# Four groups of loads behind the sums trip, and a second operand of 96 rows

## The chip, the cores and the metric

The kernel runs on one core of a Trainium2 chip. The metric is the device time of one execution in microseconds; the time of a kernel is the median of several runs. Beside it there is one profiled execution, from which every row below comes. PE is TensorE, PEld its weight loads, DVE VectorE, ACT ScalarE, POOL GpSimd, SP the engine that issues the DMAs here.

## The reference

Two layers on an image of 48 x 48 = 2304 positions with 256 channels, batch 2. Cut to the two attentions that the change touches:

```python
# layer 0, x normed by groups; 8 heads, hd = 32, values of 64
attn1 = softmax(Q1 @ K1.T * hd ** -0.5)
attn2 = softmax(Q2 @ K2.T * hd ** -0.5)
out = (attn1 - lam * attn2) @ V        # then an RMS norm and a projection
# layer 1, 4 heads of 64
logits = where(causal, q @ k.T * 64 ** -0.5, finfo.min)
attn_out = softmax(logits) @ v
# then a linear recurrence, a gate and an FFN, and a second FFN on the better half of the tokens
```

## The kernel before, in words

The program is a sequence of stages: projection, differential attention (16 pairs of batch and head), a middle stage, causal attention (2 batches of two pairs of heads), recurrence with FFN, the second FFN and the choice of tokens. The change touches the two attentions. Each is written engine by engine, with semaphores between them; the order of the work is that of the program text.

**Differential attention** (`differential_attention`). A head's 2304 queries are cut into NC = 6 chunks of T = 384, the keys into 18 steps of 128. The 96 chunks q run in a hardware loop (`Fori`) of 8 rounds with 12 chunks, two heads, written out in its body; SP's program is written out for all 96. Queries and keys are each split in a high and a low part, and the scores need three products of 32 rows, so qs and ks hold 96 rows of parts and one more row, in which the negative maximum of a query is added (L394 scores, 97 rows; L404 maxima, 96 rows). For a chunk, PE makes 36 score matmuls into three banks (`ring`), ACT takes the exponential (L502) into probs, PE multiplies by the values (L430), POOL and DVE add up the probs (L654, L601). In between PE makes the scores of a chunk ahead once more with the queries on the partitions (`max_pair`, L404), and DVE reduces them to maxima (L582); there are two buffers for these.

The sums of chunk q-1 are inverted during chunk q by a trip of four legs on SP's queue (`invert_sums`): row_sums out to memory (L348), compact in (L350), then DVE's reciprocal (L605), row_factors out (L353), and recip in twice (L357). DVE's `normalise` (L612) then makes normed, which SP stores (L363). In DVE's program L605 stands between reductions of maxima in slot 2 of the chunk.

At q % 6 == 0, ahead of trip and store, SP issues the loads of the next head (`load`): three parts for each of qs and ks and both halves, 12 loads of 288 KB, and the values, one of 576 KB. All count on one semaphore, s_ld, which PE waits for in chunk 4 of the head (slot 4) and DVE in chunk 5 (slot 2).

**Causal attention** (`causal_attention`). A pair of heads z // 6 has six query chunks, chunk c with 3 * (c + 1) steps of 128 keys. The product has two operand pairs: qa and ka with 128 rows, qb and kb with the remaining product of 64 rows; in qb and kb a 65th row, number DH = 64, adds the negative maximum. A score (`score_step`) is L1162 (128 rows) and L1163 (65 rows), on the diagonal also L1165 (mask). A maximum (`max_unit`) is L1179 (128 rows) and L1180 (64 rows: without the row of the maximum), on the diagonal L1182 (mask), reduced by DVE (L1299) from one of three banks. L1191 multiplies probs and values, with two heads in the two halves of 64 columns; L1216 sums up the same way; L1204 (`rows`) turns the maxima, with one column. DVE and ACT write the turned row into row 64 of qb (`place_row`). A planner (`plan`) spreads the 504 maxima units of later chunks over the 252 steps, two to three to a step:

```python
for lap, uz, u in todo[:n]:
    max_unit(b + lap, uz, u)
score_step(b, z, g)
for lap, uz, u in todo[n:n + 1]:
    max_unit(b + lap, uz, u)
if g > 0:
    pv_step(b, z, g - 1)
for lap, uz, u in todo[n + 1:]:
    max_unit(b + lap, uz, u)
```

Ahead of its loop of two rounds (one per batch) PE makes the 24 units of the first two chunks. DVE first sets row 64 of the four kb to one (L1289), then `ones` (L1291) and `ident_bf` (L1293); PE waits for all of these and for its first loads.

Of the kernel before, what the change touches and what calls it, by code (L numbers as in the profile page):

```python
# [6 lines left out]
F32 = mybir.dt.float32  # L7
F32R = mybir.dt.float32r
BF16 = mybir.dt.bfloat16
ALU = mybir.AluOpType  # L10
ACT = mybir.ActivationFunctionType
AX = mybir.AxisListType

P = 128
# [3 lines left out]
N = 48 * 48  # L18
T = 384
NC = N // T  # L20
SUB = T // P
NT = N // P
H0 = 8
HD = 32
VD = 2 * HD
# [213 lines left out]
def differential_attention(nc, qk_hi, qk_lo, v_rows, lambdas, ident, row_sums, row_factors, o_rows):  # L239
# [11 lines left out]
    LOADS = 2 * 2 * PARTS + 1  # L251
    PAIRS = SUB * NC

    SLOTS = 2 * STEPS + 3
# [28 lines left out]
    with ExitStack() as ctx:  # L283
        sb, ps, sem = tools(nc, ctx, "diff")
# [39 lines left out]
        with nc.Block() as block:  # L324
            @block.sync
            def _(sp):
# [7 lines left out]

                def load(n):
                    par, (b, h) = n % 2, divmod(n % HEADS, H0)
                    for j in range(2):
                        for dst, kind, parts in ((qs, 0, (qh, qh, ql)), (ks, 1, (qh, ql, qh))):
                            for r, src in enumerate(parts):
                                sp.dma_start(dst[par][j][r * HD:(r + 1) * HD, :].bitcast(F32),  # L340
                                             src[b * 2 * H0 + kind * H0 + h, j, :, :]).then_inc(s_ld[par], 16)
                    sp.dma_start(vs[par][:, :, 0, :], v_tiles[:, b * NT:(b + 1) * NT, h * VD:(h + 1) * VD]
                                 ).then_inc(s_ld[par], 16)

# [15 lines left out]
                def store(q):  # L360
                    n, c = divmod(q, NC)
                    sp.wait_ge(s_norm, q + 2)
                    sp.dma_start(o_rows[:, n + 1, c * T:(c + 1) * T], normed[:]).then_inc(s_st_o, 16)  # L363
# [4 lines left out]
                for q in range(CHUNKS):  # L368
                    if q % NC == 0:

                        sp.wait_ge(s_pv, q * BATCHES + BATCH)
                        load(q // NC + 1)
                    invert_sums(q - 1)
                    store(q - 1)
                invert_sums(CHUNKS - 1)
# [604 lines left out]
def causal_attention(nc, qk_hi, qk_lo, v_rows, ident, o_t):  # L980
# [4 lines left out]

    HN, DH = 4, C // 4
    PAIRS = HN // 2
    BANKS = 3
# [57 lines left out]
    with ExitStack() as ctx:  # L1046
        sb, ps, sem = tools(nc, ctx, "causal")
        ka = [[sb(f"ka{i}{j}", [P, N], F32R) for j in range(2)] for i in range(2)]
        kb = [[sb(f"kb{i}{j}", [DH + 1, N], F32R) for j in range(2)] for i in range(2)]
        qa = [sb(f"qa{j}", [P, N], F32R) for j in range(2)]  # L1050
        qb = [sb(f"qb{j}", [DH + 1, N], F32R) for j in range(2)]
        vs = [sb(f"vs{i}", [P, NT, 2, DH]) for i in range(2)]
# [26 lines left out]
        with nc.Block() as block:  # L1079
# [64 lines left out]
            def _(pe):  # L1144
# [23 lines left out]
                def max_unit(b, z, u):  # L1168
# [10 lines left out]
                    pe.matmul(to, qa[j][:, queries], ka[par][j][:, keys], start=True, stop=False)  # L1179
                    mm = pe.matmul(to, qb[j][0:DH, queries], kb[par][j][0:DH, keys], start=False, stop=k < c)  # L1180
                    if k == c:
# [64 lines left out]
            def _(act):  # L1246
# [4 lines left out]
                def place_row(b, z):  # L1251

                    c = z % NC
                    act.wait_ge(s_rows, b * SLOTS + z + 2)
                    act.activation(qb[1][DH:DH + 1, c * T:(c + 1) * T], misc[32:33, 0:T], ACT.Copy).then_inc(s_row, 1)

# [26 lines left out]
            def _(dve):  # L1283
# [3 lines left out]
                for par in range(2):  # L1287
                    for j in range(2):
                        ins = dve.memset(kb[par][j][DH:DH + 1, :].bitcast(F32), 1.0)  # L1289
                ins.then_inc(s_ones, 1)  # L1290
# [18 lines left out]
                def place_row(b, z):  # L1309

                    c = z % NC
                    dve.wait_ge(s_rows, b * SLOTS + z + 2)
                    dve.tensor_copy(qb[0][DH:DH + 1, c * T:(c + 1) * T], misc[0:1, 0:T]).then_inc(s_row, 1)

# [898 lines left out]
```

## Time and profile before

| what | us |
|---|---|
| median of 3 runs (6028.88 to 6040.64) | 6037.92 |
| the profiled execution | 6063.87 |
| its span, first to last instruction | 6062.1 |
| PE busy | 5460.9 (90%) |
| DVE, ACT, POOL busy | 3506.3, 2393.7, 3071.3 |
| differential attention, from SP's first load to the last chunk | 229.6 to some 3240 |
| causal attention, PE's first to last matmul | 3634.8 to 4566.7 |

Read the stages apart: the shares of busy time are means over all of them. In a window a row gives busy time of each engine and PEclk, the granted share of TensorE's clock (1.00 is 2.4 GHz, 0.50 is 1.2 GHz). In a timeline the distance between two starts says more of a matmul than its modelled duration, since matmuls overlap.

### The profile page before, as it was taken

The page shows a single profiled execution, that of the slowest core. Times are in us where ns is not written, and L with a number is a line of the kernel's source. Part 1 is how long each engine was busy: PE and PEld are TensorE (multiplying, and loading weights), DVE is VectorE, ACT ScalarE, POOL GpSimd, SP SyncE. Part 2 cuts the span into 40 slices and gives each one's busy share as a digit, 9 for nine tenths or more (in the row PEclk, how much of TensorE's full clock was granted, in tenths as well). Part 3 has the DMA queues.
Part 4 walks back from the last instruction along what each step waited for, and adds up shares of the span by engine and source line. Part 5 has one row for each costly group of instructions (what it writes and reads, how often), then busy time and mean ns, then how long its engine had stood idle before and what let it go on. Part 6 is the DMA issues. An engine that isn't in the chain of part 4 may idle for free. (4 is left out here: it accounts for less than half of the span.)

```text
span 6062.1 us, 84099 instructions
## 1 busy us (share of the span) xinstructions
PE 5460.9 (90%) x23692; PEld 3112.7 (51%) x23692; DVE 3506.3 (58%) x4330; ACT 2393.7 (39%) x5287; POOL 3071.3 (51%) x1607
## 2 busy tenths in 40 slices
PE   8799999999999999999996979999997988897970
PEld 4455555555555555555553434554554555554540
DVE  3477777777777777777774543443443444443228
ACT  3255555555555555555552211322322333332430
POOL 0198888988888988888883102544441000000001
PEclk9799999999999999999997886999998999998995
DMA  6601111101111011111013643112201000000121
GB/s 224 190 16 40 41 42 42 37 19 42 42 42 42 18 39 40 42 41 41 15 41 94 179 147 73 37 37 53 58 16 61 21 21 21 21 10 30 47 92 69
DMA packets 244613, 330.97 MB, mean 55 GB/s; under 512 B 87260, under 2 KB 224754, under 8 KB 234490
## 3 DMA queue, kind: packets, MB, share of 16 engines
q1 hardware_dynamic: 244218, 326.08, 19.4%
q8 instruction: 201, 3.29, 0.2%
q14 instruction: 194, 1.59, 0.1%
HBM read 202.49 MB, written 123.51 MB: 54 GB/s over the span
## 5 line engine op out<-in xcount | busy, mean ns | idle before, releaser
L654 POOL TENSOR_TENSOR diff_run_pool<-diff_run_pool,diff_probs 128x768 f32<-128x768 f32 x1152 | 2235.1, 1940 | 187.8 <-ACT diff_probs L502 100.6
L582 DVE TENSOR_REDUCE diff_maxes<-diff_max 128x1 f32<-128x768 f32 x1752 | 1571.7, 950 | 676.3 <-PE diff_max L404 675.5
L502 ACT ACTIVATE diff_probs<-diff_ring 128x384 f32<-128x384 f32 x3462 | 1398.8, 495 | 956.9 <-PE diff_ring L394 843.0
L430 PE MATMUL diff_out_ps<-diff_probs,diff_vs 128*64 128x384 f32 x6912 | 1272.5, 504 | 0.0
L394 PE MATMUL diff_ring<-diff_qs,diff_ks 97*128 97x384 f32 x3462 | 1076.5, 385 | 19.6 <-issue 10.1
L404 PE MATMUL diff_max<-diff_ks,diff_qs 96*128 96x384 f32 x3504 | 953.9, 354 | 98.8 <-DVE diff_maxes L582 65.0
L394 PEld LDWEIGHTS diff_ring<-diff_qs,diff_ks 97*128 97x128 f32 x3462 | 607.3, 188 | 552.1 <-issue 360.1
L430 PEld LDWEIGHTS diff_out_ps<-diff_probs,diff_vs 128*64 128x64 f32 x6912 | 453.0, 139 | 559.3 <-issue 360.5
L404 PEld LDWEIGHTS diff_max<-diff_ks,diff_qs 96*128 96x128 f32 x3504 | 613.0, 193 | 148.3 <-DVE diff_maxes L582 95.5
L2083 POOL MEMSET pick_before<- 128x128 f32 x1 | 0.2, 204 | 1311.0 <-POOLq L63 1311.0
L1299 DVE TENSOR_REDUCE causal_maxes<-causal_max 128x1 f32<-128x384 f32 x522 | 288.7, 554 | 522.2 <-PE causal_max L1180 316.4
L1377 POOL TENSOR_TENSOR causal_run_sum<-causal_run_sum,causal_probs 128x768 f32<-128x768 f32 x180 | 329.0, 1828 | 275.6 <-ACT causal_probs L1273 275.6
L1273 ACT ACTIVATE causal_probs<-causal_scores 128x384 f32<-128x384 f32 x504 | 228.4, 488 | 588.0 <-PE causal_scores L1163 400.9
L659 POOL TENSOR_TENSOR diff_row_sum<-diff_run_pool,diff_sum_dve 128x768 f32<-128x768 f32 x96 | 176.5, 1839 | 172.9 <-DVE diff_sum_dve L601 164.4
L1179 PE MATMUL causal_max<-causal_ka,causal_qa 128*128 128x384 f32 x522 | 229.2, 439 | 31.9 <-DMA causal_vs<-v_rows 28.1
L1180 PE MATMUL causal_max<-causal_kb,causal_qb 64*128 64x384 f32 x522 | 243.3, 466 | 0.0
L1191 PE MATMUL causal_out_ps<-causal_probs,causal_vs 128*64 128x384 f32 x1008 | 226.9, 531 | 0.0
L1162 PE MATMUL causal_scores<-causal_qa,causal_ka 128*128 128x384 f32 x504 | 217.4, 431 | 0.0
L601 DVE TENSOR_TENSOR diff_run_dve<-diff_probs 128x768 f32<-128x768 f32 x96 | 206.1, 2147 | 0.0
L654 POOL TENSOR_TENSOR diff_run_pool<-diff_probs 128x768 f32<-128x768 f32 x96 | 174.6, 1818 | 53.6 <-ACT diff_probs L502 46.0
L1179 PEld LDWEIGHTS causal_max<-causal_ka,causal_qa 128*128 128x128 f32 x522 | 106.0, 203 | 160.0 <-DVE causal_maxes L1299 105.0
L601 DVE TENSOR_TENSOR diff_run_dve<-diff_run_dve,diff_probs 128x768 f32<-128x768 f32 x96 | 183.0, 1907 | 0.0
(228 smaller groups left out, 5935.9 us busy)
## 6 DMA issues: line engine op xcount, KB each, us to landing
diff_qs<-qk_hi SPq DMA_DIRECT2D x68, 288.0 KB, 7.7
diff_ks<-qk_hi SPq DMA_DIRECT2D x68, 288.0 KB, 10.1
diff_recip<-row_factors SPq DMA_DIRECT2D x194, 96.0 KB, 2.7
o_rows<-diff_normed SPq DMA_DIRECT2D x97, 192.0 KB, 1.8
qk_hi<-proj_hi SPq DMA_DIRECT2D x12, 1536.0 KB, 5.8
qk_lo<-proj_lo SPq DMA_DIRECT2D x12, 1536.0 KB, 9.6
causal_qa<-qk_hi SPq DMA_DIRECT2D x120, 96.0 KB, 2.5
diff_qs<-qk_lo SPq DMA_DIRECT2D x34, 288.0 KB, 8.8
```

What stands on the lines that cost most here:

```text
L394: pe.matmul(ring[bank][:, 0:T], ks[par][j][:, g * P:(g + 1) * P], qs[par][j][:, c * T:(c + 1) * T], start=True, stop=True).then_inc(s_ring, 1)
L404: mm = pe.matmul(max_ps[u % 2][:, k, 0:T], qs[par][j][0:ROWS, c * T + s * P:c * T + (s + 1) * P], ks[par][j][0:ROWS, keys], start=True, st ...
L430: mm = pe.matmul(out_ps[VD * j:VD * (j + 1), 0:T], vs[par][:, g, j, :], probs[g % PBUF][:, j * T:(j + 1) * T], start=g == 0, stop=g == STE ...
L502: act.activation(probs[g % PBUF][:, j * T:(j + 1) * T], ring[bank][:, 0:T], ACT.Exp, scale=SCALE).then_inc(s_taken, 1)
L582: dve.tensor_reduce(maxes[side][:, row:row + 1, h], max_ps[u % 2][:, :, 0:T], AX.XY, ALU.max).then_inc(s_red, 1)
L601: dve.tensor_tensor(to[:], acc[:], probs[g % PBUF][:], ALU.add).then_inc(s_accd, 1)
L654: pool.tensor_tensor(run_pool[:], acc[:], probs[g % PBUF][:], ALU.add).then_inc(s_accp, 1)
L1179: pe.matmul(to, qa[j][:, queries], ka[par][j][:, keys], start=True, stop=False)
L1180: mm = pe.matmul(to, qb[j][0:DH, queries], kb[par][j][0:DH, keys], start=False, stop=k < c)
L1273: act.activation(probs[at % PBUF][:, j * T:(j + 1) * T], scores[(2 * at + j) % BANKS][:, 0:T], ACT.Exp, scale=SCALE).then_inc(s_exp, 1)
L1299: dve.tensor_reduce(maxes[z % 2][:, j * SUB + s:j * SUB + s + 1, k], max_ps[at % BANKS][:, 0:T], AX.X, ALU.max).then_inc(s_red, 1)
L1377: pool.tensor_tensor(to[:], acc[:], probs[at % PBUF][:], ALU.add).then_inc(s_acc, 1)
```

## The change

`load` takes a list of pieces (0: first half of qs, 1: first half of ks, 2 and 3: the second halves, 4: the values), and SP calls it in chunks 0 to 3 of a head, each time behind trip and store. The semaphore and its total stay. In the causal stage kb and qb get 97 rows: 0 to 63 as before, 64 to 95 zero, row 96 = TOP for the maximum. L1180's matmul spans 96 rows, L1163's 97. DVE sets the zero rows of the four kb and the two qb.

```diff
--- before.py
+++ after.py
@@ -250,6 +250,7 @@
     PBUF = 9
     LOADS = 2 * 2 * PARTS + 1
     PAIRS = SUB * NC
+    PIECES = (0,), (1,), (2, 3), (4,)
 
     SLOTS = 2 * STEPS + 3
     LEAD = 2 + 2 * BATCH
@@ -332,15 +333,18 @@
                 ql = qk_lo.rearrange("b (h j d) n -> (b h) j d n", j=2, d=HD)
                 v_tiles = v_rows.rearrange("(t p) c -> p t c", p=P)
 
-                def load(n):
+                def load(n, pieces=range(5)):
                     par, (b, h) = n % 2, divmod(n % HEADS, H0)
-                    for j in range(2):
-                        for dst, kind, parts in ((qs, 0, (qh, qh, ql)), (ks, 1, (qh, ql, qh))):
+                    for piece in pieces:
+                        if piece == 4:
+                            sp.dma_start(vs[par][:, :, 0, :], v_tiles[:, b * NT:(b + 1) * NT, h * VD:(h + 1) * VD]
+                                         ).then_inc(s_ld[par], 16)
+                        else:
+                            j, kind = piece // 2, piece % 2
+                            dst, parts = ((qs, (qh, qh, ql)), (ks, (qh, ql, qh)))[kind]
                             for r, src in enumerate(parts):
                                 sp.dma_start(dst[par][j][r * HD:(r + 1) * HD, :].bitcast(F32),
                                              src[b * 2 * H0 + kind * H0 + h, j, :, :]).then_inc(s_ld[par], 16)
-                    sp.dma_start(vs[par][:, :, 0, :], v_tiles[:, b * NT:(b + 1) * NT, h * VD:(h + 1) * VD]
-                                 ).then_inc(s_ld[par], 16)
 
                 def invert_sums(q):
 
@@ -366,12 +370,12 @@
                 for i, l in enumerate(lambdas):
                     sp.dma_start(lam_in[:, i, :], l.rearrange("h d -> (h d)").partition_broadcast(P)).then_inc(s_lamin, 16)
                 for q in range(CHUNKS):
-                    if q % NC == 0:
-
-                        sp.wait_ge(s_pv, q * BATCHES + BATCH)
-                        load(q // NC + 1)
                     invert_sums(q - 1)
                     store(q - 1)
+                    if q % NC < len(PIECES):
+
+                        sp.wait_ge(s_pv, q * BATCHES + BATCH)
+                        load(q // NC + 1, PIECES[q % NC])
                 invert_sums(CHUNKS - 1)
                 store(CHUNKS - 1)
                 sp.wait_ge(s_st_o, (CHUNKS + 1) * 16 + 1)
@@ -984,6 +988,7 @@
 
 
     HN, DH = 4, C // 4
+    TOP = 3 * P // 4
     PAIRS = HN // 2
     BANKS = 3
     PBUF = 6
@@ -1046,9 +1051,9 @@
     with ExitStack() as ctx:
         sb, ps, sem = tools(nc, ctx, "causal")
         ka = [[sb(f"ka{i}{j}", [P, N], F32R) for j in range(2)] for i in range(2)]
-        kb = [[sb(f"kb{i}{j}", [DH + 1, N], F32R) for j in range(2)] for i in range(2)]
+        kb = [[sb(f"kb{i}{j}", [TOP + 1, N], F32R) for j in range(2)] for i in range(2)]
         qa = [sb(f"qa{j}", [P, N], F32R) for j in range(2)]
-        qb = [sb(f"qb{j}", [DH + 1, N], F32R) for j in range(2)]
+        qb = [sb(f"qb{j}", [TOP + 1, N], F32R) for j in range(2)]
         vs = [sb(f"vs{i}", [P, NT, 2, DH]) for i in range(2)]
         probs = [sb(f"probs{i}", [P, 2 * T]) for i in range(PBUF)]
         run_sum = sb("run_sum", [P, 2 * T])
@@ -1177,7 +1182,7 @@
                     queries = slice(c * T + s * P, c * T + (s + 1) * P)
                     to, keys = max_ps[at % BANKS][:, 0:T], slice(k * T, (k + 1) * T)
                     pe.matmul(to, qa[j][:, queries], ka[par][j][:, keys], start=True, stop=False)
-                    mm = pe.matmul(to, qb[j][0:DH, queries], kb[par][j][0:DH, keys], start=False, stop=k < c)
+                    mm = pe.matmul(to, qb[j][0:TOP, queries], kb[par][j][0:TOP, keys], start=False, stop=k < c)
                     if k == c:
                         mm = pe.matmul(to, ident_bf[:], mask_q[:, s, :], start=False, stop=True)
                     mm.then_inc(s_mx, 1)
@@ -1252,7 +1257,7 @@
 
                     c = z % NC
                     act.wait_ge(s_rows, b * SLOTS + z + 2)
-                    act.activation(qb[1][DH:DH + 1, c * T:(c + 1) * T], misc[32:33, 0:T], ACT.Copy).then_inc(s_row, 1)
+                    act.activation(qb[1][TOP:TOP + 1, c * T:(c + 1) * T], misc[32:33, 0:T], ACT.Copy).then_inc(s_row, 1)
 
                 def take_out(b, z):
 
@@ -1286,7 +1291,10 @@
                 dve.sem_inc(s_norm, 1)
                 for par in range(2):
                     for j in range(2):
-                        ins = dve.memset(kb[par][j][DH:DH + 1, :].bitcast(F32), 1.0)
+                        dve.memset(kb[par][j][DH:TOP, :].bitcast(F32), 0.0)
+                        ins = dve.memset(kb[par][j][TOP:TOP + 1, :].bitcast(F32), 1.0)
+                for j in range(2):
+                    ins = dve.memset(qb[j][DH:TOP, :].bitcast(F32), 0.0)
                 ins.then_inc(s_ones, 1)
                 dve.memset(ones[:], 1.0).then_inc(s_ones, 1)
                 dve.wait_ge(s_const, 16)
@@ -1310,7 +1318,7 @@
 
                     c = z % NC
                     dve.wait_ge(s_rows, b * SLOTS + z + 2)
-                    dve.tensor_copy(qb[0][DH:DH + 1, c * T:(c + 1) * T], misc[0:1, 0:T]).then_inc(s_row, 1)
+                    dve.tensor_copy(qb[0][TOP:TOP + 1, c * T:(c + 1) * T], misc[0:1, 0:T]).then_inc(s_row, 1)
 
                 def invert(b, z, s):
```

SP's queue, chunks 0 to 3 of the third head (diff_qs00 and so on: buffers of that head's parity, first digit parity, second the half). Before, chunk 0 with what follows:

```order
L363 DMA o_rows<-diff_normed 128x384
L340 DMA diff_qs00<-qk_hi 32x2304 x2
L340 DMA diff_qs00<-qk_lo 32x2304
L340 DMA diff_ks00<-qk_hi 32x2304
L340 DMA diff_ks00<-qk_lo 32x2304
L340 DMA diff_ks00<-qk_hi 32x2304
L340 DMA diff_qs01<-qk_hi 32x2304 x2
L340 DMA diff_qs01<-qk_lo 32x2304
L340 DMA diff_ks01<-qk_hi 32x2304
L340 DMA diff_ks01<-qk_lo 32x2304
L340 DMA diff_ks01<-qk_hi 32x2304
L342 DMA diff_vs0<-v_rows 128x18x64
```

All 13 stand ahead of chunk 0's first leg. After, chunks 0 and 1 (the lines of the changed kernel; L352 and L354 are the first two legs of the trip, L367 the store):

```order
L352 DMA row_sums<-diff_sums 2x384
L354 DMA diff_compact<-row_sums 128x6
L357 DMA row_factors<-diff_compact_inv 128x6
L361 DMA diff_recip<-row_factors 64x384 x2
L367 DMA o_rows<-diff_normed 128x384
L346 DMA diff_qs00<-qk_hi 32x2304 x2
L346 DMA diff_qs00<-qk_lo 32x2304
L352 DMA row_sums<-diff_sums 2x384
L354 DMA diff_compact<-row_sums 128x6
L357 DMA row_factors<-diff_compact_inv 128x6
L361 DMA diff_recip<-row_factors 64x384 x2
L367 DMA o_rows<-diff_normed 128x384
```

Three loads now follow chunk 0's store; three follow in chunk 1, six in chunk 2 and the values in chunk 3.

DVE's preparation of the causal stage, after the change (before, the ten memsets of kb and qb are four, of 1x2304 each):

```order
L1294 MEMSET causal_kb00 32x2304
L1295 MEMSET causal_kb00 1x2304
L1294 MEMSET causal_kb01 32x2304
L1295 MEMSET causal_kb01 1x2304
L1294 MEMSET causal_kb10 32x2304
L1295 MEMSET causal_kb10 1x2304
L1294 MEMSET causal_kb11 32x2304
L1295 MEMSET causal_kb11 1x2304
L1297 MEMSET causal_qb0 32x2304
L1297 MEMSET causal_qb1 32x2304
L1299 MEMSET causal_ones 128x64
L1301 CAST causal_ident_bf<-causal_ident 128x128
```

Six memsets more stand ahead of the two instructions that PE waits for. PE's own order is the same in both kernels.

## Rows read from the trace of the kernel before

**Rows 1.** windows, one chunk each: us; busy PE, PEld, DVE, ACT, POOL; PEclk; DMA share

```profile
497.02:526.47 29.45, 29.41 (x155) 17.49 (x156) 22.80 (x24) 16.17 (x41) 26.98 (x14) 1.00 0.05 15
458.69:497.02 38.33, 31.72 (x155) 18.17 (x156) 20.23 (x25) 16.16 (x41) 26.32 (x14) 0.87 0.55 119
...
1013.32:1049.37 36.05, 32.12 (x155) 19.03 (x156) 21.59 (x25) 16.46 (x40) 26.26 (x14) 0.91 0.59 128
...
sum 592.24, PE 512.47 PEld 297.15 DVE 344.52 ACT 260.38 POOL 419.67; mean PE 32.03 PEld 18.57 DVE 21.53 ACT 16.27 POOL 26.23
```

**Rows 2.** timeline of SP's queue: start us, us to issue, line, out<-in

```profile
994.59 0.49 SPq L348 DMA_DIRECT2D row_sums<-diff_sums  x1
996.13 0.32 SPq L350 DMA_DIRECT2D diff_compact<-row_sums  x1
...
1029.20 2.39 SPq L348 DMA_DIRECT2D row_sums<-diff_sums  x1
...
1177.62 0.49 SPq L348 DMA_DIRECT2D row_sums<-diff_sums  x1
...
1206.83 7.48 SPq L348 DMA_DIRECT2D row_sums<-diff_sums  x1
1216.90 0.34 SPq L350 DMA_DIRECT2D diff_compact<-row_sums  x1
...
1229.03 0.33 SPq L363 DMA_DIRECT2D o_rows<-diff_normed  x1
1245.02 0.49 SPq L348 DMA_DIRECT2D row_sums<-diff_sums  x1
```

**Rows 3.** waits in 1196.4 to 1234.5: total us, times, longest

```profile
DVE diff_compact_inv L605 <- DMA diff_compact<-row_sums: 8.8, 1, 8.8
```

**Rows 4.** timeline behind a jump back: start us, us, [idle before <-releaser]

```profile
1014.62 0.61 PE L394 MATMUL diff_ring<-diff_qs,diff_ks 97*128 97x384 f32 x2 [1.34 <-issue]
...
1016.60 1.76 ACT L502 ACTIVATE diff_probs<-diff_ring 128x384 f32<-128x384 f32 x4 [2.79 <-PE diff_ring L394]
```

**Rows 5.** windows of the causal stage

```profile
3666.07:3768.93 102.86, 102.86 (x295) 49.16 (x294) 32.38 (x57) 19.82 (x41) 27.11 (x15) 0.61 0.16 38
3768.93:4130.41 361.48, 354.85 (x1555) 182.03 (x1553) 152.16 (x267) 107.20 (x237) 180.68 (x99) 1.00 0.14 36
3912.42:3981.66 69.24, 69.24 (x299) 34.45 (x298) 35.06 (x61) 18.88 (x41) 27.96 (x16) 1.00 0.43 103
4131.63:4175.32 43.69, 43.69 (x152) 21.38 (x151) 16.45 (x29) 9.47 (x20) 13.05 (x7) 0.76 0.51 122
```

**Rows 6.** timeline of PE in the causal stage, full clock

```profile
3995.49 0.45 PE L1162 MATMUL causal_scores<-causal_qa,causal_ka 128*128 128x384 f32 x1
3995.78 0.34 PE L1163 MATMUL causal_scores<-causal_qb,causal_kb 65*128 65x384 f32 x1
3995.95 0.34 PE L1162 MATMUL causal_scores<-causal_qa,causal_ka 128*128 128x384 f32 x1
...
3996.32 0.33 PE L1179 MATMUL causal_max<-causal_ka,causal_qa 128*128 128x384 f32 x1
3996.58 0.44 PE L1180 MATMUL causal_max<-causal_kb,causal_qb 64*128 64x384 f32 x1
3996.95 0.54 PE L1191 MATMUL causal_out_ps<-causal_probs,causal_vs 128*64 128x384 f32 x2
```

**Rows 7.** timeline of PE at the end of the causal startup, low clock

```profile
3665.46 0.69 PE L1180 MATMUL causal_max<-causal_kb,causal_qb 64*128 64x384 f32 x1
3666.07 0.69 PE L1162 MATMUL causal_scores<-causal_qa,causal_ka 128*128 128x384 f32 x1
```

**Rows 8.** timeline of the causal stage's preparation and first matmul

```profile
3623.38 1.98 DVE L1289 MEMSET causal_kb<- 1x2304 f32 x1 [0.43 <-issue]
...
3625.46 0.16 DVE L1293 CAST causal_ident_bf<-causal_ident 128x128 bf16<-128x128 f32 x1
...
3634.77 0.66 PE L1179 MATMUL causal_max<-causal_ka,causal_qa 128*128 128x384 f32 x1 [28.09 <-DMA causal_vs<-v_rows]
```

## The prediction

> **What bounds the kernel now.** I read the trace stage by stage, since the two edits lie in two different stages, and in each I asked which wait ends last.
>
> In the differential stage the loop runs over 96 chunks, six to a head. [rows 1] cut it at PE's hand-over of a finished chunk (the copy of diff_out_ps, L516). A chunk inside a head takes 29.45 us with PE busy for all of it and the clock granted in full. A chunk that begins a head takes 36 to 39 us, its mean clock is 0.86 to 0.91, and the DMA share rises from 0.05 to 0.55: this is where SP issues the next head's 13 loads. The first window of rows 1 is a normal chunk, the other 15 (two of them and the sum are shown) are all the head starts inside the loop. They come in two kinds. Where the hardware loop goes on inside its body (8 of them), the first shows 38.33 us. Where the loop also jumps back (7 of them, as at 1013.32), 36.05.
>
> [rows 2] is SP's queue. Inside a head the trip of the sums (row_sums out, compact in, factors out, recip in) starts every 29.2 to 29.45 us. At 1206.83 the first leg of the trip starts on time, 29.21 us after 1177.62, but the second starts 10.07 us later, against 1.54 after 994.59: it stands behind the 13 loads in the DMA queue. The next trip then starts at 1245.02, 38.19 us after, 8.74 too many. [rows 3] says who pays: VectorE waits 8.8 us for diff_compact, in front of its own reductions of the maxima, so PE has no bank for them and stops. At the jump back the trip is late for another reason first: it starts 34.61 us after the one before (994.59 to 1029.20), not 29.21, so 5.40 us are lost before it. [rows 4]: behind the jump ScalarE stays idle for 2.79 us and begins at 1016.60, on a score whose matmul began at 1014.62.
>
> In the causal stage PE is the bound: the long window of [rows 5] has it busy 354.85 of 361.48 us, with VectorE at 42% and GpSimd at 50%. [rows 6] is PE matmul by matmul at the full clock. Read the distance from one start to the next. Between two full-height matmuls it is 0.17 to 0.19 us (L1162 to L1163 to L1162, 128 and 65 rows; 3995.95 to 3996.32 is two of them). Before a matmul of another shape it is 0.26 (3996.32), after one 0.29 (3995.49), and with such neighbours on both sides 0.37 (3996.58). L1180 is the one with 64 rows; L1191 has 64 columns. So each change of shape costs about (0.37 - 0.18) = **0.19 us**, and L1180 makes one before itself and, unless L1191, L1204 or L1216 follows, one behind. [rows 7] is at the low clock: 0.61 from L1180 to the next; a stream takes twice 0.17 there, so a change costs 0.27.
>
> **The change part by part.**
>
> *Loads behind the sums trip.* Nothing is added; 13 issues move from ahead of trip and store to behind them, as 3, 3, 6 and 1 in chunks 0 to 3. What is removed: the 15 head starts last 592.24 - 29.45 = 562.79 us [rows 1], at 29.45 each they would last 441.75, so 121.0 us are lost. The part ahead of the trip at the jump back, 7 x 5.40 = 37.8, I leave in place: the jump is still there. That leaves **83.2 us** gained. The clock's fall at a start without a jump belongs to the removed wait (in the normal chunk it stays at 1.00), so it goes with it.
> What the groups do in their new place: SP reaches them after the store, at 1229.03, and the next trip starts at 1245.02, 16 us later [rows 2]. The 13 loads (twelve of 288 KB and one of 576) take about 0.56 x 38 = 21 us of all engines [rows 1], so the largest group, six of 288 KB, takes about 9 and is gone by then. SP has nothing else to do meanwhile, so its queue delays nobody. The first wait for them is PE's in chunk 4, slot 4, half a chunk behind the last group. Cost taken: 0; bounds: 0, and 1 us in each of the 64 chunks if the rest of a group overlaps a leg.
>
> *Padding.* Matmul counts stay. L1180 gets 96 rows; L1163 gets 97 instead of 65, and 65 rows already run at 0.18. That 96 rows count as full height I take from the nearest rows, the 65 after 128 of [rows 6]. Counted along PE's program order, the loop of the causal stage loses 826 changes of shape in both its rounds (before every L1180, and behind two of three), the startup ahead of it 48.
> 1. Steady part: of the 826, 72 lie in the first three query chunks and 35 in the two behind the jump back. The other 719 x 0.19 = **136.6 us**. PE stays the bound: the 361.48 us window holds 342 of them and shrinks to some 296, with VectorE at 152 and GpSimd at 181 [rows 5]. For VectorE's reciprocals, three in a row per chunk, I take off 3 us.
> 2. First three chunks: 102.86 us at a mean clock of 0.61. The same work in the second pair of heads takes 69.24 at the full clock [rows 5], and 72 x 0.19 less is 55.5. Does the clock come back earlier? It was low for the 31 us of the startup (L1180 at 0.69 us, [rows 7]) and for 0.78 of the 102.86, 111 us in all, although PE was busy throughout; 0.27 of every 0.61 us at an L1180 were a change of shape. In the new startup full-height matmuls stand back to back, as at the places in the first stage where the clock did return. I take it as back: **47.4 us** gained.
> 3. Startup, 31.30 us for 24 maxima units (3634.77 in [rows 8] to 3666.07 in [rows 7]): with 48 changes gone a unit takes PE 0.66 us or more at low clock, and VectorE needs about 0.6 for each, so 24 units, two turns through rows() of 2.7 and one unit's lag make about 23. Gain **8.3**.
> 4. Behind the jump back, 43.69 us at a mean clock of 0.76, so 21 low; behind a jump of the first stage it is 0.09 x 36.05 / 0.5 = 6.5 us low [rows 1], and I keep 7. Low clock costs (102.86 - 69.24) / 80 us = 0.42 per us. With 14 low us gone and 35 changes at 0.19: 5.9 + 6.7, taken as **12**.
> 5. VectorE's preparation grows from four memsets to ten. [rows 8]: each takes 1.98 us, 0.43 after the one before, for one partition; I take the same for 32, the free size being the same. Six more are 14.5 us, so the cast at 3625.46 moves to 3639.9 and PE, which waits for it, from 3634.77 (set by a load now) to 3640.2: **5.4 us lost**. Bounds: 0 if they hide, 10 if 32 partitions take half as long again.
>
> Sum: 83.2 + 136.6 - 3 + 47.4 + 8.3 + 12 - 5.4 = 279.1 us. The profiled execution took 6063.87 us (span 6062.1), 26 above the median of 6037.92; it would become 5784.8, and the median **5759**.
>
> **One rule against this.** The row first: in [rows 6] L1163 (65 rows) starts 0.17 to 0.29 behind a matmul of 128 rows, less than a weight load and a stream one after the other, so its weights came in while the other ran, although both use the same rows of the array. The Trainium skill, "TensorE: Matmul & The Clock Gate", Part 3 on packing small matmuls, says that a weight load overlaps a running matmul only when the row groups differ. By that rule 96 rows would be no better off than 64, and the padding would gain nothing; the trace speaks against it for 65 rows, and no row here has 96 next to 128. That is rival B.
>
> **The rivals.**
> - *A: the clock stays low as long as before.* For: busy matmuls did not lift it for 112 us. Then the startup and the first three chunks save 48 changes and 72 at 0.27 or less, about 31 us instead of 55.7, and the jump back 8 instead of 12: **5788**.
> - *B: 96 rows are still a shape of their own.* Against: 65 rows are not. The loads alone then, less the memsets: 83.2 - 5.4: **5960**.
> - *C: PE stops being the bound in the causal stage.* VectorE serves units and reciprocals in order with three banks; if half of the 136.6 is lost to it: **5827**. Against: the shares above.
> - *D: the trip is as slow as before*, since something else than the loads holds it: 5759 + 83: **5842**. Against: the late leg is seen only beside the loads.
> - *E, slower: the groups run into the next trip in every one of chunks 0 to 3.* Where a loaded queue catches the trip, a chunk loses 8.74 us [rows 2]; 64 chunks are 559 us: 5759 + 559 = **6318**. It makes the kernel slower from 4.4 us per chunk on, when a group lands more than some 20 us after its issue; the estimate above says 9.
>
> **How the numbers follow.** Forecast 0.62, A 0.20, B 0.05, C 0.08, D 0.03, E 0.02. Downwards the range takes the lost 5.4 us back, and the clock's fall behind the seven jumps, which rows 4 leave open: 2.79 of the 5.40 is the fetch, so up to 7 x 2.6 = 18 us, and a change priced at 0.21 (14 us): 5722. Upwards it holds A, a change priced at 0.17 (17 us), and a few us of VectorE's lag: 5812. That leaves out B, C, D and E, 0.18. A measurement of this kernel can tell about 0.2% (12 us) from no change. Faster than that are all but E: 0.97; within it 0.01; slower 0.02.
>
> **What would show it.** Right: head starts at 29.5 us, and at about 34.8 at the jump, the second leg 1.5 us behind the first in every chunk, no fall of the clock at starts without a jump; L1180's successor starting 0.18 behind it, the causal loop's steady window of 361 us near 296, the first three query chunks near 56, PE's first causal matmul 5 us later against the stage's start. Wrong: 0.37 still around L1180 (B), PE idle in waits on causal_maxes (C), a long second leg in chunks 1 to 4 (E), a clock of 0.5 for 100 us in the causal stage (A).

## The result, and the profile after

| | before | changed |
|---|---|---|
| median of runs on one chip, us | 6039.28 (6028.88 to 6051.43, 4 runs) | 5775.11 (5773.50 to 5777.92, 4 runs) |
| the profiled execution, us | 6063.87 | 5774.45 |
| its span, us | 6062.1 | 5772.7 |
| ratio, 95% interval | | 0.9562 (0.9544 to 0.9581) |

The kernel became 264 us faster. The forecast was 5759, its range 5722 to 5812.

**Differential stage.** Windows of the changed kernel, which answer to [rows 1] (us; busy PE, PEld, DVE, ACT, POOL; PEclk; DMA share, GB/s): a chunk that begins a head inside the loop's body, and two that begin one behind a jump back.

```profile
1171.66:1200.88 29.22, 29.22 (x155) 17.52 (x156) 20.24 (x25) 16.17 (x41) 27.14 (x14) 1.00 0.18 45
...
991.04:1024.64 33.60, 31.18 (x155) 18.12 (x156) 22.62 (x25) 16.28 (x40) 26.95 (x14) 0.95 0.16 40
...
2774.34:2809.33 34.99, 32.36 (x155) 19.07 (x156) 23.40 (x24) 16.49 (x41) 26.27 (x14) 0.90 0.16 38
```

The first took about 38 us before and is now like any other chunk, with the clock granted in full. The other two keep the jump's part. The timeline of SP's queue (start, us to issue) through chunk 2 of that head, with the largest group, answers to [rows 2]:

```profile
1240.56 0.50 SPq L352 DMA_DIRECT2D row_sums<-diff_sums  x1
1242.12 0.34 SPq L354 DMA_DIRECT2D diff_compact<-row_sums  x1
...
1253.41 0.33 SPq L367 DMA_DIRECT2D o_rows<-diff_normed  x1
1254.10 0.80 SPq L346 DMA_DIRECT2D diff_qs<-qk_hi  x2
...
1256.38 0.42 SPq L346 DMA_DIRECT2D diff_ks<-qk_hi  x1
...
1269.74 0.50 SPq L352 DMA_DIRECT2D row_sums<-diff_sums  x1
1271.30 0.35 SPq L354 DMA_DIRECT2D diff_compact<-row_sums  x1
```

The second leg starts 1.56 us behind the first, and six loads issued at 1254.10 are no hindrance at 1269.74. When they were done shows in windows of the same stretch (columns as above):

```profile
1258.00:1262.00 4.00, 4.00 (x22) 2.45 (x20) 3.52 (x5) 2.74 (x7) 2.86 (x3) 1.00 1.01 224
1262.00:1264.00 2.00, 2.00 (x13) 0.77 (x10) 0.85 (x1) 0.06 (x1) 1.92 (x2) 1.00 0.40 92
1264.00:1266.00 2.00, 2.00 (x11) 1.63 (x11) 1.18 (x2) 1.72 (x5) 1.92 (x2) 1.00 0.00 0
```

The DMA engines fall silent before 1264, less than 10 us after the first issue. Over the whole stage VectorE's waits for diff_compact (the lines' groups; busy us, mean ns | idle before, releaser) went from 116.8 to 32.4 us; first the kernel before, then the changed one:

```profile
L605 DVE RECIPROCAL diff_compact_inv<-diff_compact 128x6 f32<-128x6 f32 x97 | 18.6, 192 | 120.2 <-DMA diff_compact<-row_sums 116.8
```

```profile
L609 DVE RECIPROCAL diff_compact_inv<-diff_compact 128x6 f32<-128x6 f32 x97 | 18.6, 192 | 36.8 <-DMA diff_compact<-row_sums 32.4
```

**Causal stage.** The timeline of PE at the full clock, which answers to [rows 6]:

```profile
3896.86 0.34 PE L1168 MATMUL causal_scores<-causal_qb,causal_kb 97*128 97x384 f32 x1
3897.03 0.34 PE L1184 MATMUL causal_max<-causal_ka,causal_qa 128*128 128x384 f32 x1
3897.21 0.33 PE L1185 MATMUL causal_max<-causal_kb,causal_qb 96*128 96x384 f32 x1
3897.47 0.87 PE L1196 MATMUL causal_out_ps<-causal_probs,causal_vs 128*64 128x384 f32 x4
3898.27 0.45 PE L1167 MATMUL causal_scores<-causal_qa,causal_ka 128*128 128x384 f32 x1
```

From L1184 to L1185 it is 0.18 us where it was 0.26 before the 64-row matmul, and to L1196, with its 64 columns, 0.26 where it was 0.37. Windows of the stage, which answer to [rows 5] one by one, with the startup's ahead of them:

```profile
3545.96:3562.54 16.58, 14.55 (x75) 9.82 (x75) 10.41 (x22) 0.83 (x2) 0.00 (x0) 0.82 0.92 211
```

```profile
3562.54:3617.94 55.40, 55.40 (x295) 33.09 (x294) 31.58 (x58) 19.71 (x42) 27.70 (x15) 1.00 0.46 107
3617.94:3921.71 303.77, 296.17 (x1556) 178.69 (x1555) 152.95 (x267) 107.25 (x237) 181.18 (x99) 1.00 0.17 43
3738.53:3794.92 56.39, 56.39 (x299) 33.31 (x298) 34.29 (x61) 18.90 (x41) 28.37 (x16) 1.00 0.53 126
3921.71:3951.27 29.56, 29.56 (x152) 17.29 (x151) 16.09 (x29) 9.37 (x20) 13.12 (x7) 0.96 0.78 183
```

The first three query chunks went from 102.86 to 55.40 us, at PEclk 1.00 instead of 0.61. The steady window ends at the first score matmul behind the jump back, 1.2 us later than the one of [rows 5]; to the same matmul it lasted 362.7 us before, so it lost 58.9. The two chunks behind the jump back went from 43.8 (between the same two matmuls) to 29.56.

Where the 289.4 us between the two profiled executions lie: 94.4 in the differential stage, 14.7 in the causal startup, 47.5 in its first three chunks, 124.0 in its steady part, 14.2 behind its jump back, 0.8 elsewhere, and 6.2 given back ahead of PE's first causal matmul.

### The profile page after: what moved, and what is told of

Read it like the earlier page. It is cut to its first block and busy times, and to the rows that moved or that the text cites. A ratio compares the mean times of both kernels' runs of the same rounds, so it can differ in the third digit from the quotient of the medians.

```text
span 5772.7 us, 84105 instructions
## 1 busy us (share of the span) xinstructions
PE 5223.8 (90%) x23692; PEld 3069.8 (53%) x23692; DVE 3456.3 (60%) x4336; ACT 2394.0 (41%) x5287; POOL 3087.8 (53%) x1607
## 5 line engine op out<-in xcount | busy, mean ns | idle before, releaser
L434 PE MATMUL diff_out_ps<-diff_probs,diff_vs 128*64 128x384 f32 x6912 | 1253.1, 498 | 0.0
L1184 PE MATMUL causal_max<-causal_ka,causal_qa 128*128 128x384 f32 x522 | 211.5, 405 | 40.2 <-DVE causal_ident_bf L1301 34.3
L1196 PE MATMUL causal_out_ps<-causal_probs,causal_vs 128*64 128x384 f32 x1008 | 217.4, 511 | 0.0
L1167 PE MATMUL causal_scores<-causal_qa,causal_ka 128*128 128x384 f32 x504 | 195.9, 389 | 0.0
L977 POOL TENSOR_TENSOR mid_o_in<-mid_o_one,mid_o_two 128x1536 f32<-128x1536 f32 x12 | 41.2, 3429 | 262.1 <-DMA mid_o_two<-o_rows 226.2
L1184 PEld LDWEIGHTS causal_max<-causal_ka,causal_qa 128*128 128x128 f32 x522 | 100.7, 193 | 148.6 <-DVE causal_maxes L1307 86.0
L1185 PE MATMUL causal_max<-causal_kb,causal_qb 96*128 96x384 f32 x522 | 177.6, 340 | 0.0
L1168 PE MATMUL causal_scores<-causal_qb,causal_kb 97*128 97x384 f32 x504 | 170.8, 339 | 0.0
```

The lines of the kernel that those rows point to most:

```text
L434: mm = pe.matmul(out_ps[VD * j:VD * (j + 1), 0:T], vs[par][:, g, j, :], probs[g % PBUF][:, j * T:(j + 1) * T], start=g == 0, stop=g == STE ...
L1167: pe.matmul(to, ka[par][j][:, keys], qa[j][:, cols], start=True, stop=False)
L1196: mm = pe.matmul(out_ps[DH * j:DH * (j + 1), 0:T], vs[z // NC][:, g, j, :], probs[(first[z] + g) % PBUF][:, j * T:(j + 1) * T], start=g == ...
```

## The experiments

The kernels were timed in three groups (1 to 3 and 7; 4 to 6 and 8; 9 and 10), each on a chip of its own and beside the kernel before; ratios are against that. The kernel before varied more than the others, from 6044 to 6101 us in these groups, with medians of 6068.32, 6083.10 and 6059.30, all above the 6039.28 of the result. So kernels with padding are compared in us with the change. It is 5775.11, and once more, in the last group, 5773.64.

**1. The kernel before again.** One execution, for its trace.

> The kernel before once more, for a second profile. The profile of before stood 26 us above its median, that of the change 1 us below its own, so the profiles differ by 289 us and the medians by 264. If that profile was an odd one, this one has a span some 25 us shorter and shows where: the first three causal query chunks near 80 instead of 102.9 us (the clock came back sooner), or head starts with a jump back near 34 instead of 36 to 39 us. If a profile always costs the kernel before 25 us, the span is 6062 again.

6055.81 us. It was 8 us shorter than the first profile, neither 25 nor 0. The first three query chunks took 86.6 us instead of 102.9, and the two behind the jump back more than in the first profile (56.7 instead of 43.8). How long the low clock lasts in these two places changes from profile to profile.

**2 and 3. Each part alone.** The loads alone: `load` and SP's order from the change, the causal stage from before. The padding alone: the reverse.

> The loads in four groups behind the trip, without the padding. My theory: the trip waited for the loads, and each head start without a jump falls from 38 to 29.3 us, each with a jump from 36 to 39 to about 34: 94 us less in the profile, about 5945 by the medians if both parts gain what the profiles say, 5970 if the missing 25 us lie here. Rival (the trip is slow for another reason): 6039.

> The padding alone. My theory: 195 us less (the profile's share of the causal stage), 5844 by the medians; the parts do not touch, so the two gains add up to that of the change. If the missing 25 us lie here, 5870. Rival (the padding needs the new loads, for instance because the clock's state is carried over): the clock stays at half in the first three causal chunks, some 5875.

Loads alone: 5968.68 us (5945.80 to 5981.30), ratio 0.9841 (0.9807 to 0.9875). Padding alone: 5865.12 (5861.68 to 5874.33), ratio 0.9668 (0.9636 to 0.9701). Against the change, leaving the loads undone costs 90 us and leaving the padding undone 194. The differential stage of the first and the causal stage of the second have the changed kernel's times (2821.5 us from the first chunk handed over to the last against 2822.0; 8.87, 19.58 and 26.96 us for the first three query chunks against 8.85, 19.59 and 26.96). The parts add up and don't need each other. Both medians are near the upper of the two times that I expected (5970 and 5870), but the kernel before was at 6068 in this group too, so they don't say to which part the 25 us between profile and median belonged. Windows of the first kernel: the first three query chunks, and the second chunk behind the jump back.

```profile
3568.40:3643.78 75.38, 75.38 (x296) 37.46 (x295) 32.27 (x57) 19.06 (x41) 27.58 (x15) 0.89 0.22 53
4025.60:4059.32 33.72, 33.72 (x107) 16.22 (x105) 11.99 (x21) 6.75 (x14) 9.42 (x5) 0.65 0.09 24
```

The same instructions, in the same order as before, now take 75.38 us instead of 102.86 or 86.6; nothing differs but how long the clock stayed low. In the second window it went the other way, 33.72 against 24.56 in the first profile of before.

**4. The change, with L1185 back at 64 rows.** It keeps the memsets and the place of the maxima's row.

```diff
-  ... qb[j][0:TOP, queries], kb[par][j][0:TOP, keys], start=False, stop=k < c)
+  ... qb[j][0:DH, queries], kb[par][j][0:DH, keys], start=False, stop=k < c)
```

> The change with L1185's matmul over 64 rows again (rows 64 to 95 are zero, so nothing is left out), the new layout, the ten memsets and the loads kept. My theory (the change of shape is the whole gain in the causal stage): about 195 to 205 us more than the change, near 5980, with 0.37 us behind each 64-row matmul and a clock at half for 45 to 110 us at the causal stage's start. Rival (the layout or the extra memsets do something): less than 150 more.

5936.20 us (5928.59 to 5937.46), ratio 0.9772 (0.9731 to 0.9814): 161 more than the change. Its timeline of PE:

```profile
3870.43 0.34 PE L1168 MATMUL causal_scores<-causal_qb,causal_kb 97*128 97x384 f32 x1
3870.61 0.33 PE L1184 MATMUL causal_max<-causal_ka,causal_qa 128*128 128x384 f32 x1
3870.87 0.44 PE L1185 MATMUL causal_max<-causal_kb,causal_qb 64*128 64x384 f32 x1
3871.24 0.87 PE L1196 MATMUL causal_out_ps<-causal_probs,causal_vs 128*64 128x384 f32 x4
```

0.26 and 0.37 are back with nothing but the rows of this one matmul. The startup is at 31.29 us and the steady chunks at the times of before to a hundredth (43.78, 50.95). It was 44 us under the 5980 that I expected. The clock came back 47.5 us after PE's first causal matmul, not after 112 as in the first profile, and sooner behind the jump back: the first three query chunks took 75.3 us instead of 102.9 and the two behind the jump 38.5 instead of 43.8, 33 of the 44. How long the low stretch lasts is not set by the shape alone.

**5. 65 rows instead of 96.**

```diff
-  ... qb[j][0:TOP, queries], kb[par][j][0:TOP, keys], ...
+  ... qb[j][0:DH + 1, queries], kb[par][j][0:DH + 1, keys], ...
```

> The change with 65 rows in L1185 instead of 96 (row 64 is zero). My theory: more than 64 rows is full height, as L1163 with 65 showed in the kernel before, so the time is that of the change, 5775, within 5 us. Rival (the rows must reach a certain height, 96): up to 200 us more.

5776.81 us (5769.16 to 5779.70), ratio 0.9509 (0.9469 to 0.9550): the change's time. Every chunk from the second on is equal to it. So the step lies between 64 and 65 rows.

**6. 64 rows in the startup alone.** The 24 units ahead of the loop have 64 rows, all others 96.

```diff
-                def max_unit(b, z, u):
+                def max_unit(b, z, u, rows=TOP):
...
-                        max_unit(0, z, u)
+                        max_unit(0, z, u, rows=DH)
```

> The change with 64 rows in the 24 units of the causal startup alone, 96 in the loop. It tells what brings the clock back. My theory (full-height matmuls back to back bring it back): the startup takes 31.3 instead of 16.6 us at the low clock, and in the loop the clock returns within some 10 us, another 4 us: 19 more, 5794. Rival A (the clock's return is a matter of chance once the stage has begun low): the first three query chunks take up to 84 instead of 55.4 us, 5795 to 5820 and spread from run to run.

5789.92 us (5787.37 to 5795.88), ratio 0.9534 (0.9494 to 0.9574): 15 more. Windows: the startup, and the first three query chunks.

```profile
3549.43:3580.30 30.87, 28.83 (x74) 13.52 (x75) 11.47 (x22) 1.16 (x3) 0.00 (x0) 0.50 0.97 224
...
3580.30:3637.12 56.82, 56.82 (x295) 34.13 (x294) 31.43 (x57) 19.49 (x41) 27.72 (x15) 0.97 0.17 44
```

The startup runs at 0.50 throughout and takes 14.3 us more; from the first 96-row matmul on (3579.98) the clock is back after 3.4 us, and the chunks lose 1.4. From PE's first causal matmul to the end of the low clock, by the granted clock of each profile:

| kernel | rows in startup / after it | us |
|---|---|---|
| before; again | 64 / 64 | 111.8; 73.9 |
| loads alone; change with 64 rows | 64 / 64 | 47.6; 47.5 |
| 64 rows in the startup | 64 / 96 | 33.9 |
| 65 rows | 65 / 65 | 13.5 |
| padding alone; the change; again | 96 / 96 | 6.3; 6.1; 3.2 |
| experiments 7; 8; 10 below | 96 / 96 | 6.2; 6.1; 3.1 |

Four profiles with 64 rows throughout spread over 64 us; the ones with padding never passed 14 after the first matmul of full height. It is not PE's idle time: in the startup of before PE is busy for 29.26 of 31.30 us, in that of the change for only 14.55 of 16.58. In the two chunks behind the jump back the clock was low for 9, 21, 43 and 51 us with 64 rows, and for 2.4 to 4.7 us in the eight profiles with padding in the loop.

**7. Six memsets instead of ten.** Rows 64 to 96 of each kb get ones in a single memset. The rows 64 to 95 of qb stay zero, so the products are the same.

```diff
-                        dve.memset(kb[par][j][DH:TOP, :].bitcast(F32), 0.0)
-                        ins = dve.memset(kb[par][j][TOP:TOP + 1, :].bitcast(F32), 1.0)
+                        dve.memset(kb[par][j][DH:TOP + 1, :].bitcast(F32), 1.0)
```

> The change with six memsets instead of ten: the four kb get ones in rows 64 to 96 with one memset each (the rows 64 to 95 of qb are zero, so the products are the same). My theory: PE's first causal matmul waits for the ident_bf cast, which falls from 25.1 us after the stage's start to 15.5, so that the loads bound it again at about 19.4: 6 us less than the change, 5769, ratio to the kernel before 0.955. Rival: PE would have waited for its loads anyway, under 1 us.

**5766.62 us** (5763.95 to 5769.70, 5 runs), ratio 0.9502 (0.9475 to 0.9529), the fastest kernel here: 8.5 under the change's first median and 7.0 under its second, with no run of the two in common. Timelines, of VectorE and PE in the change and then here:

```profile
3521.12 1.98 DVE L1294 MEMSET causal_kb<- 32x2304 f32 x1 [8.34 <-PEq L63]
3523.62 1.98 DVE L1295 MEMSET causal_kb<- 1x2304 f32 x1 [0.52 <-issue]
...
3545.58 0.16 DVE L1301 CAST causal_ident_bf<-causal_ident 128x128 bf16<-128x128 f32 x1
...
3545.96 0.66 PE L1184 MATMUL causal_max<-causal_ka,causal_qa 128*128 128x384 f32 x1 [34.29 <-DVE causal_ident_bf L1301]
```

```profile
3522.99 1.98 DVE L1294 MEMSET causal_kb<- 33x2304 f32 x1 [8.34 <-PEq L63]
...
3537.11 0.16 DVE L1300 CAST causal_ident_bf<-causal_ident 128x128 bf16<-128x128 f32 x1
...
3541.40 0.66 PE L1184 MATMUL causal_max<-causal_ka,causal_qa 128*128 128x384 f32 x1 [27.88 <-DMA causal_vs<-v_rows]
```

In the change PE follows the cast by 0.4 us, 25.5 us after SP's first load of the stage; here it is 19.1 us, and a load releases it, as before the change [rows 8]. With ten memsets VectorE is last and costs 6.4 us; with six it is done 4.3 us ahead of the load.

**8. One group of 13, behind the store of chunk 0.**

```diff
-    PIECES = (0,), (1,), (2, 3), (4,)
+    PIECES = (0, 1, 2, 3, 4),
```

> All 13 loads behind the store of chunk 0, in one group. My theory: they begin 24 us into chunk 0 and take some 20, so they end 5 us into the time of chunk 1's first leg; that trip is late by 3 to 6 us, of which VectorE's slack takes 2: 1 to 4 us in each of 16 heads, 5790 to 5840. Rival (only the place behind the store matters): 5775.

5807.52 us (5806.32 to 5814.35), ratio 0.9567 (0.9527 to 0.9608): 32 more than the change. Between the two profiles this stage alone accounts for 38. SP's queue:

```profile
1211.86 0.89 SPq L346 DMA_DIRECT2D diff_qs<-qk_hi  x2
...
1217.52 0.43 SPq L340 DMA_DIRECT2D diff_vs<-v_rows  x1
1227.82 1.54 SPq L352 DMA_DIRECT2D row_sums<-diff_sums  x1
1232.83 0.34 SPq L354 DMA_DIRECT2D diff_compact<-row_sums  x1
```

The first leg comes 16 us after the first issue and the second 5.0 after the first. The 13 are just not through: they need some 19 us (from 1211.86 to 1.5 us ahead of the second leg). The chunk takes 30.6 to 34.8 us instead of 29.2 to 29.5, in all 16 heads. This is rival E's mechanism at a small size.

Against the padding alone (5865.12), where the same 13 stand ahead of the trip, this kernel is 58 us faster. The stage takes 2914.4 us there, 2860.2 here and 2822.0 in the change. So with one group the place alone earns over half of what the edit to the loads earns.

**9 and 10. The change again, and its four groups ahead of the trip.**

```diff
-                    invert_sums(q - 1)
-                    store(q - 1)
                     if q % NC < len(PIECES):
 
                         sp.wait_ge(s_pv, q * BATCHES + BATCH)
                         load(q // NC + 1, PIECES[q % NC])
+                    invert_sums(q - 1)
+                    store(q - 1)
```

> The changed kernel once more, unaltered, as the measure of its own spread on this chip and as what the kernel beside it is compared with. Expected: 5770 to 5780 us, z-chunks of the causal stage as in its first profile (8.9, 19.6, 27.0 for the first three), head starts at 29.2 to 29.5 without a jump and 32 to 35.3 with one.

> The changed kernel with the same four groups in chunks 0 to 3, but each ahead of trip and store instead of behind them. Theory 1 (what matters is how much is queued when the trip's first leg comes): SP issues a group at the chunk's start and reaches the first leg at once when the sums are there; a group of three loads of 288 KB lasts some 4.5 us, one of six about 9 (estimated from 21 us for all 13), and if the first leg comes about 10 us into the chunk all of them are gone by then: within 0.2% of the change, second leg 1.55 us behind the first everywhere, 5765 to 5785 us. Theory 2 (place matters: whatever stands ahead of the trip in a chunk holds it): the second leg is late in proportion to the group, by some 2 us with three loads and some 5 with six, and since the slack of the trip in a chunk is about 4 us (the run with one group behind the store lost up to 4 us per head only), the chunk with six loads and the chunk at a head's start lose 1 to 4 us each: 5790 to 5850 us. Slower than the kernel before in neither.

The change again: 5773.64 us (5773.37 to 5776.95), ratio 0.9521 (0.9484 to 0.9558). The groups ahead of the trip: 5774.35 (5772.07 to 5777.80), ratio 0.9522 (0.9485 to 0.9559). No difference between the medians. SP's queue around the largest group:

```profile
1054.75 0.80 SPq L346 DMA_DIRECT2D diff_qs<-qk_hi  x2
...
1056.98 0.42 SPq L346 DMA_DIRECT2D diff_ks<-qk_hi  x1
1065.23 0.50 SPq L352 DMA_DIRECT2D row_sums<-diff_sums  x1
1066.98 0.34 SPq L354 DMA_DIRECT2D diff_compact<-row_sums  x1
```

From the chunk's start to the first leg there are 10.5 us, and six loads are gone in less. The second leg is 1.75 behind, with no loss. The division into groups earns all that the edit to the loads earns, without the move; the move without the division earns over half of it (experiment 8). Behind the division the move adds nothing that the medians show. One thing differs between the two profiles: the seven starts behind a jump take 34.9 to 35.9 us here, 35.3 in the mean, against 34.2 in the change again. The stage is 5.6 us longer for it (2829.4 against 2823.8) and the rest of that execution 6.9 shorter, so whether the move is worth a few us at the jumps stays open.

## Why the prediction was right, and where it was not

| term | predicted gain, us | profile to profile |
|---|---|---|
| head starts | 83.2 | 94.4 |
| steady causal part | 136.6 - 3 | 124.0 |
| first three query chunks | 47.4 | 47.5 |
| startup | 8.3 | 14.7 |
| behind the jump back | 12 | 14.2 |
| VectorE's preparation | -5.4 | -6.2 |
| elsewhere | 0 | 0.8 |
| sum | 279.1 | 289.4 |

*What bounds the kernel* held. The padding moved PE's time one to one, with PE still busy 296.17 of 303.77 us (rival C is out). The second leg is 1.54 to 2.07 us behind the first in all 97 trips. Experiments 2 to 4 show each part to be the cause of its share.

*Head starts.* The mechanism held: the trip was late because of the loads queued ahead of it. The place did not matter once they came in groups (experiment 10); with one group it did (experiment 8). The term was 11 too small, for two reasons. I took 29.45 us as a normal chunk's length from one that followed a disturbed start. In the trace four chunks behind such a start take 29.45, and all from the fifth on 29.20, until the next one (29.43, 29.46, 29.44, 29.47, then 29.19 behind the start that ends at 1382.2). Heads that begin inside the body no longer have a disturbed start, so their start and the four chunks behind it gained 0.25 each, some 9 us in seven heads. And the jump's starts last 32.0 to 35.3 us, 34.0 in the mean, not the 34.8 I kept: 6 us. Two chunks ahead of a jump, of 30.4 and 32.3 us, took 4 back. The prediction called 2.79 us at the jump "the fetch"; no run shows what ScalarE or PE waits for there.

*Steady part.* 719 changes gave 124.0 us, 0.172 each, where I had 0.19. Two kinds hide in the mean. Taken from the starts of PE's matmuls in the steady windows, a unit between the second score matmul and L1191 (one change) went from 0.641 to 0.448 us from the start of L1184 (before, L1179) to the third start behind it, 0.193 saved. One between L1191 and a score (two changes) went from 1.026 to 0.638, 0.194 for each. These I had right. But a unit on the diagonal, with its bf16 mask L1187 behind it (two changes), went from 0.903 to 0.619: 0.142 for each. From L1185 to the mask it saves 0.195, ahead of L1185 0.088, and behind the mask nothing, since 0.267 to L1196 stand in both kernels. The diagonal's rows were in the trace of before, and I read none of them. Of the 3 us taken off for VectorE about 2 came: PE's idle time in the window grew from 6.6 to 7.6 us, and there are two such windows.

*Clock.* That the low stretch ends in the new startup (against rival A) is what the trace shows; experiment 6 ties it to the height of the matmuls. PE was not busy throughout before, as I wrote: 2.0 of the startup's 31.3 us were idle; but so are 2.0 of the new one's 16.6. What I had wrong is what the first profile stood for. Its 112 us after the first causal matmul was one draw; others were 74, 47.6 and 47.5. The median missed by 16 us, although the sum against the profile came out 10 on the other side. The step that failed is carrying the 26 us between the profiled execution and the median over to the changed kernel: its profiled time is 0.7 from its median. I take those us for part of the low stretches, which the change removes, so that against that median the clock's term was worth less than against that profile; no trace of an execution near 6038 is there to show it. Nor is 6038 firm: the medians of the kernel before in the three later groups are 6059 to 6083, around the profiled 6063.87. In the last group, with both kernels on one chip, the medians are 285.7 us apart, not 264, and the sum of 279.1 is 7 from that. The runs bear the clock's part in the spread out only partly: the kernel before spreads over 23 to 56 us in a group of runs and the loads alone over 36, those with padding over 4 to 13; but the one with 64 rows in experiment 4 spread over only 9, so I don't call the spread's cause shown.

*Startup.* It went to 16.58 us, or 15.3 when the clock rose sooner. I had priced all of it at the low clock; it rises 6 us into it, and the rest of the 24 units goes at full speed.

*VectorE's preparation.* 1.98 us for 32 partitions as for one was right. The gap behind a memset is 0.52 in the new mix, not 0.43, which is the missing 0.8 us.

*The rule set against it.* The row: L1185 with 96 rows starts 0.18 us behind a matmul of 128 rows which uses the same rows of the array, and its weights load while that one runs (L1184's matmul is the one at 3897.03 above):

```profile
3897.04 0.19 PEld L1185 LDWEIGHTS causal_max<-causal_kb,causal_qb 96*128 96x128 f32 x1
```

The Trainium skill, "TensorE: Matmul & The Clock Gate", Part 3, says in its list that a weight load overlaps running matmuls only when the row groups differ. The trace does not agree. (The same Part also lets a load go ahead that targets the background weight buffer; that would fit.) The Trainium skill, "TensorEngine Tiling (Array Packing)", Key Properties, says that a change of tiling mode drains the array; its Available Configurations list modes of 128, 64 and 32 rows. The step between 64 and 65 rows (experiment 5) fits that, though no run shows the mode itself; the page has no price, and the runs give 0.14 to 0.19 us for a change. The Trainium skill, "DMA: Bandwidth & Descriptors", Queues, rings and completion order, has each ring's descriptors consumed in order. Experiments 8 and 10 agree: the trip's second leg is 5.0 us behind the first where 13 loads are still running, and 1.75 where the group is through.

## What to carry to other kernels

Before moving a transfer out of the way of a small one, ask how much stands in the queue when the small one comes. Groups that are through by then cost nothing on either side of it; one group that isn't costs on either side, less behind it. A float32 matmul of 64 rows among matmuls of full height is dearer than one of 65 to 97: pad it with zero rows, and set them and their neighbours by one memset. When a profile holds a stretch at the low clock, take a second profile before pricing it, and don't carry the distance between profile and median over to the changed kernel unless something shows what it consists of.

## What the runs showed of the hardware

- A change between 64 rows and full height costs 0.19 us at the full clock between float32 matmuls and 0.14 in a group that ends with a bf16 one. 65, 96, 97 and 128 rows can follow each other at 0.18 us.
- At the start of the causal stage, with 64-row matmuls in between, PE stayed at 0.50 for 47 to 112 us, although it was busy for 93% of the startup and all the time behind it; with full height it was granted 1.00 within 14 us of the start, mostly 3 to 6. In the two chunks behind the jump back the low clock lasted 9 to 51 us against 2.4 to 4.7.
- A memset of 2304 float32 takes 1.98 us on 1, 32 and 33 partitions.
- Six loads of 288 KB are through in less than 10 us at 224 GB/s, and 13 (4.0 MB) take some 19.
- One disturbed chunk (by a late trip, or by a jump back) costs more than its own delay: the four chunks behind it are 0.25 us longer each. Why the fifth drops to 29.20 was not tried.
- A jump back of the hardware loop keeps costing 2.8 to 6.1 us per jump over a chunk of 29.2 in the change's profile (up to 6.7 in experiment 10's), and 0 to 6.8 us of low clock. Its cause was not tried either.
